# Half of the layer-0 products in three rounded passes, and three chunks per tile scaled in PSUM by ScalarE, in a three-layer interaction network

## The reference, cut to what matters

```
x0 = input                                  # 512 x 64 fields x 16 elements
x_vec = x0
for W, b in ((W0, b0), (W1, b1), (W2, b2)):
    z = einsum('bhd,bfd->bhfd', x_vec, x0)  # products of each row of x_vec with each field
    x_vec = einsum('oc,bcd->bod', W, z.reshape(B, h * f, d)) + b[None, :, None]
    outs.append(x_vec.sum(axis=2))
return concatenate(outs, axis=1)            # 512 x 384
```

## Time and profile before

| | |
|---|---|
| median of 3 runs | 1140.29 us (1138.67 to 1140.75) |
| the profiled execution | 1139.53 us, of which its span is 1137.7 us |
| TensorE matmul busy | 1096.1 us, 96% |
| VectorE busy | 868.1 us, 76% |
| GpSimd busy | 840.5 us, 74% |
| ScalarE busy | 453.2 us, 40% |

### The profile page before, as it was taken

How to read it: one execution, slowest core, us unless ns; L and a number is a source line. 1 busy time by engine, 2 the same in 40 slices (tenths; PEclk the granted TensorE clock), 3 DMA queues, 4 the chain that set the end, 5 groups by cost and what they waited for, 6 DMA issues and landing times.

```text
span 1137.7 us, 16831 instructions
## 1 busy us (share of the span) xinstructions
PE 1096.1 (96%) x4589; PEld 775.6 (68%) x4589; DVE 868.1 (76%) x3002; ACT 453.2 (40%) x1532; POOL 840.5 (74%) x762
## 2 busy tenths in 40 slices
PE   2899999999999999999999999999999999999996
PEld 2477666676668666666668666766667766766776
DVE  3356978888794888979794797978887588888991
ACT  2244434444341443434352343434443253443550
POOL 3766796979784797878876688787978479697551
PEclk9989999999999999999999999999999999999998
DMA  7861423314051141514142051423313133240000
GB/s 248 249 165 40 93 72 68 91 27 123 24 122 44 34 115 23 124 35 112 54 93 56 17 115 51 95 70 72 94 29 102 35 81 85 41 111 15 1 1 28
DMA packets 112350, 86.89 MB, mean 76 GB/s; under 512 B 75136, under 2 KB 75776, under 8 KB 112128
## 3 DMA queue, kind: packets, MB, share of 16 engines
q1 hardware_dynamic: 109376, 75.27, 27.6%
q10 hardware_dynamic: 2880, 10.55, 2.6%
HBM read 14.75 MB, written 0.79 MB: 14 GB/s over the span
## 4 chain that ended last, share of the span: by engine, by line
PE 83%; DVE 11%; DMA 3%; issue 2%; POOL 1%; ACT 0%; SPq 0%; POOLq 0%
PE y L644 54%; PE l L656 19%; DVE acc L584 8%; PE xt L679 5%; PE l2p L691 3%; DMA xg<-in_r_input_dram 2%; DVE bd L551 2%; DMA z<-xg 1%; DVE x1l L559 1%; PE l2p L668 1%; PE xt L661 1%; PE y L733 0%; PE l L652 0%; POOL z L337 0%; DVE acc L582 0%
## 5 line engine op out<-in xcount | busy, mean ns | idle before, releaser
L584 DVE SCALAR_TENSOR_TENSOR acc<-y,x0t,acc 128x128 f32<-128x128 f32 x2560 | 699.2, 340 | 201.6 <-PE y L644 198.9
L490 ACT ACTIVATE prod<-y,x0t 128x128 f32<-128x128 f32 x1280 | 367.6, 371 | 607.0 <-PE y L644 573.8
L644 PE MATMUL y<-w1h,x1h 128*128 128x512 f32 x1024 | 509.3, 497 | 6.2 <-DVE acc L584 4.3
L644 PE MATMUL y<-w1h,x1l 128*128 128x512 f32 x1024 | 404.3, 395 | 0.0
L644 PE MATMUL y<-w1l,x1h 128*128 128x512 f32 x1024 | 403.7, 394 | 0.0
L348 POOL TENSOR_TENSOR pacc<-pacc,prod 128x512 f32<-128x512 f32 x192 | 247.1, 1287 | 183.8 <-ACT prod L490 183.8
L337 POOL TENSOR_TENSOR z<-z,xg 128x512 f32<-128x512 f32 (+1 forms) x272 | 353.0, 1303 | 25.7 <-DMA z<-xg 25.5
L644 PEld LDWEIGHTS y<-w1h,x1h 128*128 128x128 f32 x1024 | 193.4, 189 | 136.5 <-issue 60.3
L656 PE MATMUL l<-z,w0t 128*128 128x512 f32 x512 | 262.6, 594 | 2.7 <-POOL z L337 2.7
L644 PEld LDWEIGHTS y<-w1l,x1h 128*128 128x128 f32 x1024 | 193.6, 189 | 81.1 <-issue 54.3
L644 PEld LDWEIGHTS y<-w1h,x1l 128*128 128x128 f32 x1024 | 192.6, 188 | 44.1
(11 more groups left out here) (50 smaller groups left out, 278.4 us busy)
## 6 DMA issues: line engine op xcount, KB each, us to landing
z<-xg SPq DMA_DIRECT2D x512, 128.0 KB, 2.4
xg<-in_r_input_dram SPq DMA_DIRECT2D x32, 128.0 KB, 3.8
w2t<-in_L_rec_W_dram ACTq DMA_DIRECT2D x8, 512.0 KB, 12.4
gram<-in_L_rec_W_dram ACTq DMA_DIRECT2D x8, 512.0 KB, 8.6
z<-xg SPq DMA_DIRECT2D x16, 192.0 KB
gram<-in_L_rec_W_dram ACTq DMA_DIRECT2D x1, 2048.0 KB, 7.9
out_dram<-z SPq DMA_DIRECT2D x4, 192.0 KB, 2.1
b1r<-in_L_rec_b_dram ACTq DMA_DIRECT2D x1, 64.0 KB, 10.0
```

What stands on the lines that cost most here:

```text
L490: last = nc.scalar.activation(prod[:, h % HSLOTS, k, :], y[c % YB][:, k * O:(k + 1) * O], ACT.Copy, scale=x0t[:, j, f:f + 1])
L584: ins = nc.vector.scalar_tensor_tensor(out=to, in0=of, scalar=x0t[:, j, f:f + 1], in1=b1r[:] if m == 0 else to, op0=ALU.mult, op1=ALU.add)
L644: ins = nc.tensor.matmul(to, stationary, moving, start=(first and k == 0), stop=(last and k == 2))
```

## The change

Two edits are made together.

Of the 16 full-width layer-0 steps, the eight even ones (PARTED) are computed in three passes of rounded operands instead of one float32 matmul. ScalarE makes the upper part zh five steps ahead, VectorE the rest zl three steps ahead; each has two buffers. The weights of these steps are split in the preparation. To make room, z has 6 slots instead of 9. `part_upper` and `scale` below are ScalarE's, `part_lower` and the piece with `y_scaled` VectorE's, the piece with `by_parts` TensorE's.

Of the chunks that VectorE sums, chunks 3, 9 and 15 of each tile (3, 6, 9 and 15 in the last group) are multiplied by ScalarE in place in PSUM, and VectorE adds the 512-wide block in one instruction.

```diff
-ZSLOTS = 9
+ZSLOTS = 6
+PARTED = tuple(range(0, ZT - 1, 2))
+ZHSLOTS = 2
+SCALED = (3, 9, 15)
+SCALED_LAST = (3, 6, 9, 15)
+PART_UPPER_AT, PART_LOWER_AT = ([AHEAD_AT[t] - k for t in PARTED] for k in (5, 3))
...
+            def part_upper(n, t):
+                i = PN * n + PARTED.index(t)
+                act.wait_ge(z_made, ZT * n + t + 1)
...
+                nc.scalar.copy(zh[:, i % ZHSLOTS, :], z[:, zslot(t), :]).then_inc(zh_made, 1)
...
+            def scale(tile, j, c):
+                act.wait_ge(y_made, CHUNKS * tile + c + 1)
+                for k in range(CF):
+                    f = CF * c + k
+                    of = y[c % YB][:, k * O:(k + 1) * O]
+                    last = nc.scalar.activation(of, of, ACT.Copy, scale=x0t[:, j, f:f + 1])
+                last.then_inc(y_scaled, 1)
...
+            def part_lower(n, t):
+                i = PN * n + PARTED.index(t)
+                dve.wait_ge(zh_made, i + 1)
+                nc.vector.tensor_tensor(zl[:, i % ZHSLOTS, :], z[:, zslot(t), :],
+                                        zh[:, i % ZHSLOTS, :].bitcast(F32), ALU.subtract).then_inc(zl_made, 1)
...
+                if c in scaled_in(tile):
+                    dve.wait_ge(y_scaled, scaled_at(tile, c))
+                    dve.wait_ge(acc_step, added(tile, SUMMED[m - 1]))
+                    to = acc[:, j % 2].rearrange("p k o -> p (k o)")
+                    nc.vector.tensor_tensor(to, y[c % YB][:], to, ALU.add).then_inc(acc_step, 1)
+                    return
...
+                if t in PARTED:
+                    i = PARTED.index(t)
+                    pe.wait_ge(zl_made, PN * n + i + 1)
+                    by_parts(l0[:], zh[:, (PN * n + i) % ZHSLOTS, :], zl[:, (PN * n + i) % ZHSLOTS, :], w0h[:, i, :],
+                             w0l[:, i, :], t == 0, False, False).then_inc(z_used, 1)
+                    return
```

More of the change, by code:

```diff
@@ L175, in cin_kernel @@
         prod_made = sem("prod_made")
+        y_scaled = sem("y_scaled")
         pool_step = sem("pool_step")
@@ L205, in parted @@
         def parted(what, r):
-            return what == "w1" or (what, r) == ("w0", W0_STEPS - 1)
+            return what != "l0"
         def parted_in(steps):
@@ L224, in z_rows, with in_last, scaled_in, add_steps @@
             return P if t < ZT - 1 else ZCOPIES * ZLAST
-        def tile_added(tile):
-            return SN * tile + 2 * SN
+        def in_last(tile):
+            return isinstance(tile, int) and tile >= LAST_TILES
+        def scaled_in(tile):
+            return SCALED_LAST if in_last(tile) else SCALED
+        def add_steps(scaled, upto):
+            return sum(1 if c in scaled else CF for c in SUMMED if c <= upto)
+        SN = add_steps(SCALED, CHUNKS)
+        def added_before(tile):
+            if in_last(tile):
+                return SN * LAST_TILES + SN + add_steps(SCALED_LAST, CHUNKS) * (tile - LAST_TILES)
+            return SN * tile + SN
+        def added(tile, c):
+            return added_before(tile) + add_steps(scaled_in(tile), c)
+        def tile_added(tile):
+            return added_before(tile + 1)
+        def scaled_at(tile, c):
+            before = len(SCALED) * tile
+            if in_last(tile):
+                before = len(SCALED) * LAST_TILES + len(SCALED_LAST) * (tile - LAST_TILES)
+            return before + scaled_in(tile).index(c) + 1
         def x2_ready(tile):
@@ L475, in body @@
                             quarter_out(n // QG)
+                    if e in PART_UPPER_AT and kind != "last":
+                        part_upper(n + 1, PARTED[PART_UPPER_AT.index(e)])
                     if e == LEFT_PARTS_AT and kind != "last":
@@ L503, in _ @@
                 act.wait_ge(prep_made, turned_in(PREP[:k]) + 1)
[L504 to L507, removed]
+                if what == "w0" and r < W0_STEPS - 1:
+                    nc.scalar.copy(w0t[:, 2 * r:2 * r + 2, :],
+                                   y[bank][:].rearrange("p (t o) -> p t o", o=O)[:, 1:4:2, :])
                 part, of = weights(w1h, what, r, bank, slice(0, z_rows(ZT - 1)))
@@ L573, in add_fields @@
                     dve.wait_ge(x2_made, x2_ready(tile - 2))
+                if c in scaled_in(tile):
[4 more added lines that the diff above has]
+                    return
                 dve.wait_ge(y_made, CHUNKS * tile + c + 1)
+                after_scaled = m > 0 and SUMMED[m - 1] in scaled_in(tile)
                 for k in range(CF):
@@ L577, in add_fields @@
                     to, of = acc[:, j % 2, k, :], y[c % YB][:, k * O:(k + 1) * O]
-                    if m > 0 and k % 2 == 0:
-                        dve.wait_ge(acc_step, SN * tile + (SN + CF * (m - 1) + k + 2))
+                    if after_scaled and k == 0:
+                        dve.wait_ge(acc_step, added(tile, SUMMED[m - 1]))
+                    elif m > 0 and not after_scaled and k % 2 == 0:
+                        dve.wait_ge(acc_step, added(tile, SUMMED[m - 1]) + (k + 2 - CF))
                     if m == 0 and k > 0:
@@ L602, in body @@
                         own_rows(n * TILES + j, j)
+                    if e in PART_LOWER_AT and kind != "last":
+                        part_lower(n + 1, PARTED[PART_LOWER_AT.index(e)])
                     if e == LEFT_LOWER_AT and kind != "last":
@@ L613, in _ @@
                 if what == "l0":
+                    if r in PARTED:
+                        part_lower(0, r)
                     if r == ZT - 1:
                         left_lower(0)
-                    continue
-                if not parted(what, r):
                     continue
@@ L701, in chunk @@
                 else:
-                    value = SN * tile + (SN + CF * SUMMED.index(before) + CF) - (SN if late else 0)
-                    pe.wait_ge(acc_step, value)
+                    pe.wait_ge(acc_step, added(tile - 1 if late else tile, before))
                 cols = slice(j * P, (j + 1) * P)
```

23 lines of the change are left out of this document (20 added, 3 removed).

## The result

The changed kernel takes 1152.95 us (median of 4, 1151.59 to 1154.18), the one before 1140.24 (median of 4, 1138.67 to 1140.75). The ratio is 1.0109, 95% interval 1.0096 to 1.0123: slower by 1.1%, where 1153 was predicted. The profiled execution took 1153.88 us, its span is 1152.2.

The account below looks back on a forecast made before the run. TensorE bounds on average (busy 96%), with VectorE also full in a 14.25 us stretch per group. 1139.5 - 20.8 gain + 32.9 stalls + 1.0 ends = 1152.6, median 1153; range 1126 to 1161, the forecast's own 1145 to 1157.

Parts of the forecast that it names:

- The stretch: Between two groups' layer-0 steps, 14.25 us with TensorE and VectorE full: first layer-0 step 2.35 us later, 14 changes, 32.9 us.
- The walk: Step-by-step working through the group change, chunk 57 to zl of t = 0, ending with TensorE's layer-0 step at 472.9.
- nothing differs: Assumption that up to chunk 57 the old kernel's clock still holds, VectorE being ready for that chunk at 458.5.
- the middle value 1.0: Assumed time in us of one VectorE lower part (zl), the middle of 0.76 and 1.26.
- The gain: TensorE's saving from rounded layer-0 steps: 0.17 us a step, 1.4 us a group, 20.8 us over 15 groups.
- the passes keep 0.229 throughout: Bracketed case for TensorE's matmul passes beside layer 0: no slower pace there, saving 0.20 us a rounded step.
- Past this point I find no further wait: After a group's first layer-0 step TensorE waits no more; the next lower part (t = 2) is ready in time.
- 0 (-1.5 to +1.5): Last group's net change in us: VectorE's load falls, but scaled chunks return banks late, about what TensorE waited before.
- The turnaround of a bank: Last group: a scaled chunk's PSUM bank is back after 2.96 us, while four chunks take 2.76 us.
- + 0.5: Cost in us allowed for the first group's changes; the preparation had the same figure, with 0 to 2.5 as its range.
- VectorE arrives in time: Rival at the group change: zl of t = 0 ready before step 9, kernel faster, 1120 with no stall; chance 0.30.
- Lower parts and GpSimd delay each other more broadly: Rival: lower parts take 1.5 us or more, GpSimd's products 0.26 later; 1173, partly 1162; chance 0.08.

Follow-up runs that it names:

- e2: Changed kernel with no chunk scaled, only the eight rounded layer-0 steps: 1145.18 us, ratio 1.0060 to the kernel before.
- e3: Changed kernel with layer-0 step t = 0 kept in float32, the other seven even steps rounded: 1132.61 us, ratio 0.9948 to the kernel before.
- e5: Changed kernel with upper and lower part of t = 0 two chunks earlier: 1153.48 us, ratio 1.0119 to the kernel before.
- e7: Changed kernel with t = 0 in float32, chunks 57, 63 and 3 unscaled, nothing scaled in the last group: 1125.11 us, ratio 0.9869.
- e8: e7 with chunk 51 of each group unscaled too: 1120.61 us, ratio 0.9830 to the kernel before.
- e6: Changed kernel with chunks 57, 63 and 3 at the group change summed by VectorE as before, unscaled: 1152.84 us, ratio 1.0108.
- e4: Changed kernel with no chunk scaled in the last group: 1151.59 us, ratio 1.0103 to the kernel before.
- e9: Changed kernel with t = 0 in float32, seven rounded steps and no chunk scaled anywhere: 1117.52 us, ratio 0.9805 to the kernel before.

## Why the prediction was right, and where it was not

*The stretch, right in mechanism and size.* The first layer-0 step came 2.19 us later (predicted 2.35), and the wait recorded before it was 1.7 (predicted about 1.5). e2 and e3 show that it is the lower part of t = 0. Its place counts too: two chunks earlier it left 1.02 of the 2.19 us at the stretch (e5), though not in the time of the kernel.

*Its parts were off.* VectorE idled 0.34 and 0.41 us for the two scalings, where 0.9 and 0.64 were worked out. ScalarE was on time (chunk 57 scaled at 529.16, old clock 459.32, predicted 459.41); it was VectorE that came later to chunk 57, at 459.01 instead of 458.5. The walk took it that up to there "nothing differs", and held the waits for scalings in the other tiles to be hidden. VectorE has such waits in every tile, and the one for chunk 51 was not hidden: e7 and e8 show that it makes VectorE 0.47 us late at bd and TensorE 0.26 at step 0. The lower part took 1.15 here and 1.16 on average, not the middle value 1.0. So the scaled chunks in the stretch cost little net, as e6 shows, and the lower part nearly all.

*The gain, a little better.* It was 0.20 to 0.21 a step instead of 0.17: the case "the passes keep 0.229 throughout" that the prediction put in brackets. Fourteen groups cost 14 x 0.60 = 8.3 us, where 14 x (2.35 - 1.38) = 13.5 was forecast. Two small slips in the working offset each other: 0.87 less 0.69 is 0.18 a step, not 0.173, and the terms of the walk end at 472.93, a stall of 2.40, not 2.35.

*"Past this point I find no further wait" held in the changed kernel.* Where the stretch is shorter, bd can meet GpSimd's product and take 1.2 to 1.55 us instead of 0.41, and TensorE waits 0.77 (e3) or 0.43 (e5) at t = 2.

*The last group, the term "0 (-1.5 to +1.5)", was mis-sized: +2.9 us.* 1.8 of it is the scaling there, 0.2 the change ahead of it (e4). The turnaround of a bank, 2.96 against 2.76 us, was worked out, and then set off against waits of before. It shows in the time per tile: the layer-2 products stand 12.70 us apart in the changed kernel (1106.50 to 1119.20) and 12.09 in e4 (1105.37 to 1117.46). The other 0.9 is the clock.

*The first group, "+ 0.5", was mis-sized in this trace.* Rows of TensorE in the changed kernel, then the window that follows:

```profile
59.23 0.47 PE L734 MATMUL y<-w1h,x1h 128*128 128x512 f32 x1 [1.74 <-DVE x1l L638]
70.91 0.77 PE L734 MATMUL l<-zh,w0h 128*128 128x512 f32 x1 [2.85 <-DVE zl L614]
71.48 0.63 PE L734 MATMUL l<-zh,w0l 128*128 128x512 f32 x1
71.90 0.63 PE L734 MATMUL l<-zl,w0h 128*128 128x512 f32 x1
```

```profile
70.91:78.91 8.00, 8.00 (x34) 6.56 (x35) 5.38 (x12) 4.01 (x12) 8.00 (x7) 0.82 0.52 132
```

TensorE stood for 2.85 us at its first layer-0 step, and the granted clock over the 8 us behind it was 0.82; the kernel before had no such wait, and 1.00 in the 8 us from its first layer-0 step at 69.09. By these figures that clock costs 8 x 0.18, some 1.4 us. e4, which is the same program up to the last group, waited only 1.38 us there, had 1.00 behind it, and took 70.6 us, 0.3 more than before. So the size of this term differs from one execution to the next, and 73.4 is at its upper end.

*The sum* came out within 0.1 us by cancelling errors. In the trace the 14 groups cost 8.3 us where 13.5 was forecast. Preparation, first and last group cost 0.2 + 3.1 + 2.9 = 6.2, where 0.5 + 0.5 + 0 less the first group's gain of 1.4 was forecast, -0.4. That slower is right, and by which wait, the runs bear out; the exact figure is luck.

*The rival "VectorE arrives in time"* fails for the changed kernel, though its price with no stall, 1120, is near what a kernel without the stall takes: e9, with neither the lower part of t = 0 nor the scaling, takes 1117.52, with seven steps at 0.21 instead of eight at 0.17. The scaling "well under 1.15 us" that the rival asked for didn't come: four pieces took 1.09 to 1.17 us. What the Trainium skill's page "ScalarE: Activation LUTs" says of ScalarE writing faster to PSUM than to SBUF (it stands in Step-by-step: what each stage is for) agrees in direction, 349 against 381 ns a piece, and is too little for it. *"Lower parts and GpSimd delay each other more broadly"* was half there: lower parts took from 0.68 to 1.81 us and GpSimd's products 1.41 instead of 1.30, yet only one step a group waited in the changed kernel; in e3 and e5 a second one did, behind bd and GpSimd. The rule of the Trainium skill quoted for it ("SBUF — State Buffer", Who interferes with whom) agrees with the lower part's 1.16 beside 0.68 at its shortest. The 131 ns a matmul of the Trainium skill's "TensorE: Matmul & The Clock Gate" (Back-to-back issue gap) shows in no run: passes stay at 0.229 us at full clock.

*What stays open.* The scaling costs 7.8 us on top of e2 by the medians (1152.95 - 1145.18). 0.27 a group is 3.8 and the last group's 2.0 make 5.8; the rest is first group and clock, which I can't divide. No run moved the first layer-0 step behind step 9, or bd away from the product beside which it stands; the two would show whether the eighth rounded step can be had without a stall.

## What to carry to other kernels

Before work is moved to an engine with room on average, look for the stretch in which it has none: here 14.25 us of 63 with both engines full decided a group, and one 1.15 us instruction placed in it ate the gain of all eight rounded steps. Moving that instruction two chunks forward gave nothing in the end, because another one became longer; leaving it out gave 1153 to 1133 us, and leaving out the "relief" by a third engine as well gave 1117.5. A wait ahead of such a stretch isn't hidden either: chunk 51's, four steps ahead, cost 0.26 us a group. A hand-over through a further engine shortens the receiver's work but lengthens the time for which a PSUM bank is held, so with few banks it must be priced as turnaround and not as busy time (2.96 against 2.76 us by the working here; what the rows show is 12.70 against 12.09 us a tile).

## What the runs showed of the hardware

- ScalarE in place in PSUM, four 128x128 pieces: 1.09 to 1.17 us, mean 349 ns a piece; into SBUF 381 ns in the same kernel. A scaled hand-over so costs 1.1 us of latency for 0.41 us of VectorE's time.
- The 128x512 subtraction of two SBUF operands takes 0.68 us at its shortest, 1.16 on average and 1.81 at most beside GpSimd's work, and GpSimd's product beside one took 1.73 us instead of 1.29. VectorE's bd, by contrast, fell from 980 ns on average to 695. At one place of e3 it took 0.41 us in four groups and 1.2 to 1.55 in ten, with starts of bd and of GpSimd's product 0.01 to 0.02 us apart in a group of either kind.
- TensorE's granted clock fell to 0.82 over the 8 us after a wait of 2.85 us, passes then standing 0.42 us apart instead of 0.23 (rows 71.48 and 71.90), the lower of its two levels (1.2 and 2.4 GHz). After e5's wait of 4.99 us it was 0.67 over 8 us. After the wait of 1.72 us at the group change shown above it was 1.00 over 8 us; after e2's first wait of 2.38 us and e6's of 2.22 us it was 1.00 too, and after e6's wait of 1.80 us it was 0.79. So the length of the wait alone does not sort these cases. The same final product took 15.9 to 17.5 us from one kernel to the next; the windows above have 16.61 at 0.87 and 17.51 at 0.82.
